# A ring of four for the kept edge units, and the broadcast operand first in the attention products

## The reference, cut to what matters

```python
w = jnp.einsum('ehd,ehd->eh', q[e_dst], k[e_src])
mx = jax.ops.segment_max(w, e_dst, num_segments=n)
ex = jnp.exp(w - mx[e_dst])
den = jax.ops.segment_sum(ex, e_dst, num_segments=n)
attn_w = ex / (den[e_dst] + 1e-16)
msgs = attn_w[:, :, None] * v[e_src]
agg = jax.ops.segment_sum(msgs, e_dst, num_segments=n)
```

```python
e = (x_dst - x_src) @ theta_w.T + x_src @ phi_w.T
e = jax.nn.relu(_bn(e, bn0_g, bn0_b))
e = e @ fc1_w.T
e = jax.nn.relu(_bn(e, bn1_g, bn1_b))
agg = jax.ops.segment_sum(e, dst, num_segments=n)
x = agg / jnp.maximum(cnt, 1.0)[:, None]
return jax.nn.relu(x + h)
```

## Time and profile before

| | us |
|---|---|
| median of 3 runs | 14954.79 |
| lowest and highest run | 14942.3, 14955.02 |
| the profiled execution | 14914.23 |
| its span, first to last instruction | 14912.4 |
| kv pass, from to | 7890 to 10510 |
| edge_spread, first to last quarter's statistics | 13362.0 to 14120.5 |
| edge_mean, first to last quarter's addition | 14155.3 to 14876.6 |

### The profile page before, as it was taken

The page is one execution under the profiler, slowest core; times in us unless marked ns, Lnnn a source line. Parts: engine busy times, 40 slices in busy tenths (PEclk is TensorE's granted clock), DMA queues, the critical chain, the costliest instruction groups (busy, mean ns, idle before and its releaser), DMA issues. The chain is left out here.

```text
span 14912.4 us, 95989 instructions
## 1 busy us (share of the span) xinstructions
PE 3867.0 (26%) x15751; PEld 2525.5 (17%) x15850; DVE 7009.2 (47%) x10781; ACT 2521.3 (17%) x6154; POOL 8357.2 (56%) x7838
## 2 busy tenths in 40 slices
PE   2011122223211222326920000000421111127666
PEld 1011011222211122223420000000211111113322
DVE  8673355556444555552034555555532222234454
ACT  0411122233212223320000000000000000004454
POOL 0116777777577777770017777777157777750012
PEclk9997565666655665657955555555655555558788
DMA  0002544444336434454703633333126433344444
GB/s 2 12 27 57 69 84 90 96 96 102 68 73 83 90 90 96 101 91 165 259 26 91 96 98 98 98 98 99 16 79 91 111 105 105 104 105 159 146 171 148
DMA packets 840654, 1414.44 MB, mean 95 GB/s; under 512 B 191956, under 2 KB 623802, under 8 KB 827672
## 3 DMA queue, kind: packets, MB, share of 16 engines
q0 software_dynamic: 277856, 659.70, 22.2%
q10 hardware_dynamic: 448192, 336.76, 8.3%
q1 hardware_dynamic: 114552, 417.44, 8.1%
HBM read 1058.01 MB, written 355.29 MB: 95 GB/s over the span
## 5 line engine op out<-in xcount | busy, mean ns | idle before, releaser
L851 POOL DMA_INDIRECT ring<-gat_table,index x3640 | 4056.4, 1114 | 1172.0 <-issue 1041.1
L851 POOL DMA_INDIRECT ring<-kv_table,index x1820 | 2030.2, 1115 | 577.8 <-issue 524.3
L851 POOL DMA_INDIRECT ring<-b_table,index x1820 | 1730.9, 951 | 670.0 <-issue 516.8
L982 PE MATMUL pairs<-hot_lo,hot_hi 128*128 128x128 f32 x6272 | 949.9, 325 | 1234.2 <-ACT hot_lo L1012 1232.7
L1076 DVE TENSOR_TENSOR prod<-ring,p 128x1848 f32<-128x1848 f32 (+1 forms) x390 | 820.3, 2103 | 721.7 <-DVEq L107 682.0
L982 PEld LDWEIGHTS pairs<-hot_lo,hot_hi 128*128 128x128 f32 x6272 | 923.7, 238 | 1287.4 <-issue 1285.9
L1012 ACT ACTIVATE hot_lo<-hot_lo,wt 128x128 f32<-128x128 f32 x3136 | 934.3, 387 | 1167.5 <-remote 1009.8
L1642 DVE TENSOR_TENSOR tb<-bt,att 128x1792 f32 x130 | 263.2, 2024 | 1663.7 <-DVEq L107 1663.7
L976 PE MATMUL pairs<-nil 128*128 128x512 bf16 x686 | 341.4, 596 | 2675.6 <-ACT dstage L1021 2629.6
L1125 ACT ACTIVATE p<-x 128x84 f32<-128x84 f32 (+1 forms) x390 | 114.2, 293 | 5220.4 <-DVE x L1072 5220.4
L1664 PE MATMUL bt<-ident,ring 128*128 128x128 f32 x1820 | 417.3, 421 | 1932.1 <-PEq L107 1932.1
(11 more groups left out here) (372 smaller groups left out, 8955.0 us busy)
## 6 DMA issues: line engine op xcount, KB each, us to landing
dense_weights<-dstage ACTq DMA_DIRECT2D x196, 1024.0 KB
mat<-dense_weights SPq DMA_DIRECT2D x98, 1568.0 KB
kept<-tb ACTq DMA_DIRECT2D x132, 896.0 KB, 3.8
layer_out<-kept SPq DMA_DIRECT2D x130, 896.0 KB
at<-kept SPq DMA_DIRECT2D x130, 896.0 KB
ring<-gat_table,index POOLq DMA_INDIRECT x3640
ring<-kv_table,index POOLq DMA_INDIRECT x1820
ring<-b_table,index POOLq DMA_INDIRECT x1820
```

What stands on the lines that cost most here:

```text
L851: pool.indirect_dma_start(self.ring[:, r * UG + i, :], None, self.table, bass.IndirectOffsetOnAxis(self.index[:, half, at:at + 1], 0)).the ...
L982: mm = pe.matmul(self.ps[:, b, i * P:(i + 1) * P], self.hot_hi[:, 4 * b + i, :], self.hot_lo[:, 4 * b + i, :], start=False, stop=False, sk ...
```

## The change

The kept units get a buffer of their own, kept_ring, of RU = 4 units, in place of the two slots inside other buffers. Two units are loaded ahead of the loop, and the loop body handles four units, in slots 2, 3, 0, 1; the trip count is the one that the gather passes use (32: 4 x 32 + 2 = 130 units). The buffers own and prod move into k.out, and fold, the square of the means at the end of `edge_spread`, into kept_ring. An own batch now stands before each of the first seven rounds of four units. `edge_mean`'s loops on PE and DVE go by band as before.

```diff
-    def __init__(self, k, s, kept, coef, slots):
-        self.k, self.kept, self.coef, self.slots = k, kept, coef, slots
+    def __init__(self, k, s, kept, coef):
+        self.k, self.kept, self.coef = k, kept, coef
+        self.slots = s.sb("kept_ring", [P, RU, S * W7])
...
     def prime(self, eng):
-        eng.sem_inc(self.tb_free, 2)
+        eng.sem_inc(self.tb_free, RU)
...
         with self.few(sp):
-            with sp.Fori(0, self.pairs(sp)) as i:
-                for h in range(2):
-                    claim(sp, self.tb_free)
-                    u = (2 * i + h).with_bounds(min_val=0, max_val=CAP - 1)
-                    sp.dma_start(self.slots[:, h * S * W7:(h + 1) * S * W7],
-                                 self.kept[ds(u, 1), :, :].rearrange("g p c -> (g p) c")).then_inc(self.loaded[h], 16)
...
+            for r in range(2):
+                fetch(r, r)
+            with sp.Fori(0, self.rounds(sp)) as i:
+                for r in range(RU):
+                    fetch((r + 2) % RU, RU * i + r + 2)
```

In the attention passes three DVE instructions get their operands in the other order, so that the one with the repeated values is the first:

```diff
-                dve.tensor_tensor(by_head(prod[:, :, :]), by_head(got[:, :, 0:VB]),
+                dve.tensor_tensor(by_head(prod[:, :, :]),
                                   weight[:, 0:UG, :].unsqueeze(3).broadcast_to([P, UG, heads, dim + 1]),
-                                  ALU.mult).then_inc(ga.used, 1)
+                                  by_head(got[:, :, 0:VB]), ALU.mult).then_inc(ga.used, 1)
...
-                return (lambda: dve.tensor_tensor(keys4, keys4,
-                                                  qt[:, :, :].unsqueeze(1).broadcast_to([P, S, B7, VB]), ALU.mult),
+                return (lambda: dve.tensor_tensor(keys4, qt[:, :, :].unsqueeze(1).broadcast_to([P, S, B7, VB]), keys4,
+                                                  ALU.mult),
```

More of the change, by code:

```diff
@@ L1754 @@
 class KeptUnits:
-    def __init__(self, k, s, kept, coef, slots):
-        self.k, self.kept, self.coef, self.slots = k, kept, coef, slots
+    def __init__(self, k, s, kept, coef):
+        self.k, self.kept, self.coef = k, kept, coef
+        self.slots = s.sb("kept_ring", [P, RU, S * W7])
         self.r4 = s.sb("r4", [P, 2 * S, QW])
-        self.loaded = [k.sem(f"tb{h}_in") for h in range(2)]
+        self.loaded = [k.sem(f"tb{h}_in") for h in range(RU)]
         self.tb_free, self.r4_free, self.relued = k.sem("tb_free"), k.sem("r4_free"), k.sem("relued")
@@ L1797, in edge_spread @@
         s = k.sub(st)
-        source = KeptUnits(k, s, kept, coef, flat2(k.out[:, :, :]))
-        stats, fold = s.sb("stats", [P, CAP * 2 * S, 2, 3]), s.sb("fold", [P, CAP * 2 * S, 2])
-        own, prod = s.sb("own", [P, W7]), s.sb("prod", [P, W7])
+        source = KeptUnits(k, s, kept, coef)
+        stats = s.sb("stats", [P, CAP * 2 * S, 2, 3])
+        fold = flat2(source.slots[:, :, :])[:, 0:CAP * 4 * S].rearrange("p (g h) -> p g h", h=2)
+        own, prod = (flat2(k.out[:, i * B7:(i + 1) * B7, :]) for i in range(2))
         pad_sums = s.sb("pad_sums", [P, NB, 2])
@@ L1841, in _ @@
             with source.few(pe):
-                last = source.pairs(pe)
+                last = source.rounds(pe)
+                for u in range(2):
+                    unit()
                 with pe.Fori(0, NB):
                     own_batch()
-                    unit()
-                    unit()
+                    for u in range(RU):
+                        unit()
                 with pe.Fori(NB, last):
-                    unit()
-                    unit()
+                    for u in range(RU):
+                        unit()
         @block.vector
@@ L1871, in own_batch @@
                 for q in range(2):
-                    c(dve.tensor_tensor(prod[:, :], part, prod[:, :] if q else pads[:, ds(b * W7, W7)], ALU.mult))
-                    c.go(dve.tensor_reduce(flat2(pad_sums[:, ds(b, 1), q:q + 1]), prod[:, :], AX.X, ALU.add))
+                    c(dve.tensor_tensor(prod, part, prod if q else pads[:, ds(b * W7, W7)], ALU.mult))
+                    c.go(dve.tensor_reduce(flat2(pad_sums[:, ds(b, 1), q:q + 1]), prod, AX.X, ALU.add))
                 c(dve.drain())
@@ L1877, in _ @@
             with source.few(dve):
-                last = source.pairs(dve)
+                last = source.rounds(dve)
                 source.prime(dve)
@@ L1884, in _ @@
                 c.reset()
+                for u in range(2):
+                    unit(u)
                 with dve.Fori(0, NB) as i:
                     own_batch(i)
-                    unit(2 * i)
-                    unit(2 * i + 1)
+                    for u in range(RU):
+                        unit(RU * i + u + 2)
                 with dve.Fori(NB, last) as i:
-                    unit(2 * i)
-                    unit(2 * i + 1)
+                    for u in range(RU):
+                        unit(RU * i + u + 2)
                 c(dve.drain())
@@ L2135, in edge_mean @@
         with ExitStack() as st1:
-            source = KeptUnits(k, k.sub(st1), kept, coef, at)
+            source = KeptUnits(k, k.sub(st1), kept, coef)
             e1 = k.sub(st1).ps("e1", [P, 2 * S, 512])
@@ L2145, in _ @@
                 with source.few(act):
-                    with act.Fori(0, source.pairs(act)):
-                        source.act_unit(act, 0)
-                        source.act_unit(act, 1)
+                    source.act_units(act, (0, 1))
+                    with act.Fori(0, source.rounds(act)):
+                        source.act_units(act, (2, 3, 0, 1))
             @block.tensor
```

42 lines of the change are left out of this document (25 added, 17 removed).

## The result

The changed kernel takes 14378.93 us (median of four runs, 14375.51 to 14384.36), against 14948.55 us for the kernel before, run beside it (four runs, 14920.12 to 14955.02). The ratio is 0.9623, with a 95% interval of 0.9606 to 0.9639. The median fell by 569.6 us; the prediction had 566 us and a time of 14390 us. In the profiled executions the spans are 14377.1 and 14912.4 us, 535.3 us apart; the one before took 14914.23 us and so lay 34 us under its median.

The account below looks back on a forecast made before the run. A load wait, and PE's clock falling in it, bound edge_spread and edge_mean. Gains of 315 and 251 us, 0 for the swap, made 566; 14955 - 566 = 14389, forecast as 14390 us, range 14300 to 14500.

Parts of the forecast that it names:

- the forecast's own bounds: Whole kernel: 14320 us with no slow clock and pauses half covered, 14463 with a costly swap and longer pauses.
- The bound: edge_spread and edge_mean: a wait for a load, 4.56 us from issue to use, and PE's clock falling in it.
- The nine quarters ahead: Ring of four: ScalarE wants a freed slot some nine quarters after release, 6.8 us against 4.56 from issue to use.
- what is left of ScalarE's waits: Both stages: waits fall from 382 and 362 us; the rest are for r4 buffers, short and even.
- The pace of a quarter: PE at full clock sets 0.75 us in edge_spread, 390 us; waiting for DVE's bank makes 0.78 in edge_mean, 406 us.
- The pauses: DVE's own batches in edge_spread, six at 8.9 us, 53 us; dve_rows in edge_mean, six at 9.7 us, 58 us.
- the 6 us for the hand-overs: edge_mean: a band's hand-over and count cost about 1 us a band, 6 us in all.
- Rival B: Both stages: PE's clock stays mixed at 0.81 and 0.87, +91 and +42 us, 14523 us; chance 0.10.
- rival E: Both stages: PE stays on 1.2 GHz throughout, 1.5 us a quarter, slower than before at 15122 us; chance 0.02.
- rival F: Both stages: the ring does not run ahead, so no change, 14955 us; chance 0.03.
- The swap: Attention passes' products with the broadcast operand first: taken as 0, with bounds of -11 to +37 us.
- That the holds stay: kv pass: gathers that meet L1076 stay held, 1.9 us, since L1082 with two dense operands holds them too.

Follow-up runs that it names:

- e8_split: Changed kernel with DVE's own batches in edge_spread and dve_rows in edge_mean cut into pieces between units; 14282.47 us in one run.
- e7_bank3: Changed kernel where DVE in edge_mean hands back a bank one quarter earlier, so PE may be three banks ahead; 14336.64 us in one run.
- e6_kv_psum: Changed kernel with the kv pass's p, prod and qt in PSUM and prod's halves added to acc in turn; 14065.11 us, 0.9428 of the kernel before.
- e4_pe_filler: Kernel before with four more unused matmuls per pair of units on PE in edge_spread; 14805.47 us in one run, against 14924.84 for the kernel before.

## Why the prediction was right

**The time.** 14390 against 14378.93 us, inside the forecast's own bounds of 14320 to 14463. The gain in the two stages was 563.2 us, not 566; the median of before, run again, was 14948.55 and not 14954.79. From these two the time would be 14385, and the last 6 us are less than the runs of the kernel before differ by. That the sum came within 3 us of the stages' gain has some luck in it, by the terms below.

**The bound.** It was the load wait, as the earlier trace rows showed: with depth two and all else as in the changed kernel, 368.7 us of wait and 748.8 us of stage stand there again. The nine quarters ahead, 6.8 us against 4.56, no run measures by themselves; that a third slot is nearly enough fits them. One sign did not come as said: what is left of ScalarE's waits was to be short and even, and 45 of the 60.1 us in edge_spread are seven waits of 6.4 us.

**The pace of a quarter.** 0.75 us in edge_spread stands in the weight loads, and `e8_split` fits it over the whole stage: 409.4 us, of which 10.5 are PE's own batches, leave 399 for 520 quarters, 0.77 each with what is left of the pauses. 0.78 in edge_mean was right in its cause (`e7_bank3`) and a little large: four quarters take 3.09 us, so 520 take 402 us, not 406.

**The pauses, the term with the larger miss in it.** The prediction counted six behind the first statistics, as in the kernel before. There are seven: the change puts two units ahead of the first own batch, as its ScalarE listing shows, so the first pause lies behind the first statistics too. Each costs (448.9 - 390) / 7 = 8.4 us, not 8.9. The slow clock fits that: it lasts 4.4 us in the pause shown (13525.07 to 13529.50) and not 5.4, which is 0.5 us less at half speed. Seven at 8.9 would have made 452, six at 8.4 would have made 440; six at 8.9 gave 443, and 448.9 was measured. The step that failed is the count, by one, and the shorter pause made up for less than half of it. In edge_mean the six pauses come to (467.7 - 402 - 6) / 6 = 10.0 us, where 9.7 was said; the 6 us for the hand-overs are the prediction's, and no run measures them. There the quarter was put too high and the pause too low, and the sum of 470 was off by 2.

**The clock.** Rival B (it stays mixed) and rival E (1.2 GHz throughout) fall with 0.97 and 0.95, and rival F (the ring does not run ahead) with the waits that are gone. The Trainium skill's "TensorE: Matmul & The Clock Gate", section "A second HAM failure mode: psum-queue depth-cycling", would have small pauses between banks make the clock swing. edge_mean has a small gap of PE in every quarter, 0.77 - 0.75 = 0.02 us, and with these in place `e8_split` ran the stage at 0.99. So the loss from 1.00 to 0.95 goes with the long pauses. The trace does not agree with it for gaps of this size, and says nothing on others.

**The swap.** 0 was right, within (0.9988 to 1.0006) x 14918 = -18 to +9 us. The lower bound of -11 and the upper of +37 from hot_hi and hot_lo were wider than was needed: the rows of after have 2084 and 2143 ns, those of before, so it makes no difference to DVE which of the two operands is the broadcast. That the holds stay was right; the prediction had it from a likeness of two rows, and `e6_kv_psum` shows the reason. The Trainium skill's "SBUF — State Buffer", section "Who interferes with whom", says that a VectorE instruction with at most one SBUF input does not contend with GpSimd outside its two-port modes, and that one with two does with a GpSimd instruction that reads SBUF. The trace agrees with both halves: 1.84 and 2.35 us beside two SBUF inputs, 0.95 beside one. Read strictly, the rule also gives the 0 for the swap.

**The kv pass** was said to take 2620 us again, in a stretch of that length. By its gathers it took 2594.3 before and 2596.4 after.

**What stays open.** The two gat passes together took 29 us more in the kernel after than in the one before, whose instructions there differ in the operands' order alone. The traces show a single long wait of POOL in each pass where the time goes, 27.8 and 13.6 us before, 37.8 and 30.6 after. In the second pass it is 13.6 and 14.1 us in the two kernels with neither half of the change (`before` and `e4_pe_filler`) and 24.9 to 30.6 in the ten others, with one profile of each. Why was not tried.

## What to carry to other kernels

Where a stage loads into as many slots as it computes from, look at how the release of a slot stands to the time from issue to use: one slot more (here a third, worth 292 us in one stage and 241 in the other) brought nearly all, and it paid twice, since PE's clock had fallen in the wait. Before swapping operands for the sake of a hold on POOL, ask how many of them lie in SBUF: the order changed nothing here, and one operand in PSUM took the hold away. When the waits for data were gone, the next cost was the long job that the consuming engine does in one piece; cutting it up was worth 40 us of 449.

## What the runs showed of the chip that was not expected

- Loads of 0.9 and 0.6 MB in pairs, with several units in flight, kept 409 GB/s for 380 us, above the 371 and 391 of the earlier trace rows, while a statistics instruction of DVE took its usual 632 ns and PE's clock was 0.98.
- Adding work shortened a stage: 50% more matmuls on PE, none of them used, took 104 us off 758.5, with the clock at 0.98 in place of 0.81 and the long waits for loads as before.
- The hold on POOL is longer at the key product (2.35 us for a gather that needs 0.95) than at the product with the weights (1.84), though both DVE instructions take 2.14. Both gathers end 0.82 us behind the instruction; the first starts 0.61 us into it, the second 1.12. What the hold costs depends on where in the product the gather begins.
- DVE's additions in the kv pass became a little cheaper with one input in PSUM, 1.15 us in place of 1.21 and 1.22.
